# Mamba layer: the skip term as a matmul with a diagonal, row normalisation and state sum on ScalarE, another form for the low row part

## The reference, cut to what matters

```python
x = x + _L0_attn_ref(_layernorm(x), ...)
# inside: xn = (x - mu) * rsqrt(var + 1e-5) * gamma + beta; result = x + mamba_f(xn) + mamba_b(xn reversed) reversed
def _mamba(x, in_w, conv_w, conv_b, xproj_w, dt_w, dt_b, A_log, D, out_w):
    u, z = split(x @ in_w.T)
    u = silu(causal_conv4(u) + conv_b)
    x_dbl = u @ xproj_w.T                      # 8 columns dt, 16 columns B, 16 columns C
    dt = softplus(x_dbl[..., :8] @ dt_w.T + dt_b)
    A = -exp(A_log)
    h[t] = exp(dt*A) * h[t-1] + dt * B * u     # per channel and state n
    y[t] = sum_n h[t, n] * C[t, n] + u * D     # u * D is the skip term
    return (y * silu(z)) @ out_w.T
```

## Time and profile before

| | us |
|---|---|
| median of 3 runs | 2815.53 |
| lowest and highest | 2811.09, 2817.47 |
| the profiled execution, device time | 2811.5 |
| its span in the trace | 2809.7 |
| Mamba layer in it | about 24 to 1137 |

### The profile page before, as it was taken

The page is one execution under the profiler, slowest core; times in us unless marked ns, Lnnn a source line. Parts: engine busy times, 40 slices in busy tenths (PEclk is TensorE's granted clock), DMA queues, the critical chain, the costliest instruction groups (busy, mean ns, idle before and its releaser), DMA issues. The chain is left out here.

```text
span 2809.7 us, 46598 instructions
## 1 busy us (share of the span) xinstructions
PE 2401.2 (85%) x14880; PEld 1568.5 (56%) x14880; DVE 2138.4 (76%) x3085; ACT 1455.2 (52%) x2617; POOL 1191.9 (42%) x864
## 2 busy tenths in 40 slices
PE   2778878778887877799779999699999989978997
PEld 0233333333333332577578888466666767767776
DVE  3899999999999999577555555588888867764555
ACT  2666666666666774466332222466666646642010
POOL 4566667666666667333300000455555533231000
PEclk9899999999999999899789999899999999988999
DMA  2000000000000000200000000000000010000000
GB/s 84 1 0 0 1 0 1 1 1 0 0 0 0 0 1 0 63 12 12 22 1 1 1 0 0 6 0 0 0 0 0 1 48 11 11 4 1 11 7 12
DMA packets 35414, 22.17 MB, mean 8 GB/s; under 512 B 22710, under 2 KB 34017, under 8 KB 34801
## 3 DMA queue, kind: packets, MB, share of 16 engines
q1 hardware_dynamic: 35312, 20.98, 2.9%
HBM read 18.87 MB, written 2.10 MB: 7 GB/s over the span
## 5 line engine op out<-in xcount | busy, mean ns | idle before, releaser
L784 POOL TENSOR_TENSOR m_hc<-m_h,m_cs 128x1024 f32<-128x1024 f32 x256 | 603.2, 2359 | 351.9 <-DVE m_h L706 344.6
L706 DVE TENSOR_TENSOR_SCAN m_h<-m_da,m_pdb 128x1024 f32<-128x1024 f32 x256 | 585.1, 2286 | 23.5 <-DVE m_pdb L661 5.0
L456 PE MATMUL m_py<-m_hc,ident 128*128 128x512 f32 x1024 | 514.6, 627 | 4.2 <-DVE m_y L670 2.1
L579 ACT ACTIVATE m_da<-m_dt,m_aneg 128x508 f32<-128x508 f32 x512 | 337.8, 709 | 47.8 <-POOL m_dt L753 46.1
L661 DVE TENSOR_TENSOR m_pdb<-m_du,m_pdb 128x1024 f32<-128x1024 f32 x256 | 314.8, 1230 | 42.7 <-POOL m_du L760 11.4
L456 PEld LDWEIGHTS m_py<-m_hc,ident 128*128 128x128 f32 x1024 | 202.2, 200 | 213.6 <-issue 174.6
L594 ACT ACTIVATE m_cs<-m_pc 128x512 f32<-128x512 f32 x256 | 150.5, 588 | 219.7 <-PE m_pc L446 219.6
L442 PE MATMUL m_pdb<-m_bcrow,m_sel 96*128 96x512 bf16 x256 | 101.8, 397 | 171.8 <-DVE m_h L706 170.8
L1391 ACT ACTIVATE c_act_of<-c_pg 128x512 f32<-128x512 f32 x144 | 86.2, 598 | 237.3 <-PE c_pg L212 237.3
L1759 POOL TENSOR_TENSOR d_pr<-d_pr,d_rden 128x512 f32<-128x512 f32 x128 | 133.3, 1041 | 177.2 <-DVE d_rden L1690 177.2
L1037 ACT ACTIVATE x_prT<-x_pt 77x512 f32<-77x512 f32 x256 | 137.8, 587 | 130.6 <-PE x_pt L939 129.5
(11 more groups left out here) (257 smaller groups left out, 5373.7 us busy)
## 6 DMA issues: line engine op xcount, KB each, us to landing
cw_gu<-in_C_gu SPq DMA_DIRECT2D x1, 2304.0 KB
x<-in_x SPq DMA_DIRECT2D x8, 256.0 KB, 4.9
fw_w<-in_F_w SPq DMA_DIRECT2D x1, 2048.0 KB
out_x<-x SPq DMA_DIRECT2D x8, 256.0 KB, 2.3
bm_mrow<-in_B_mrow SPq DMA_DIRECT2D x1, 1232.0 KB, 6.5
x_ctxT<-in_B_ctxT SPq DMA_DIRECT2D x32, 38.5 KB, 1.8
x_mask<-in_B_mrow SPq DMA_DIRECT2D x32, 38.5 KB, 2.8
x_ctxT<-in_E_ctxT SPq DMA_DIRECT2D x32, 38.5 KB, 1.8
```

The lines of the kernel that those rows point to most:

```text
L456: ins = mm(py[:, c, :], S.ident[:, :], hc[n % BUF][:, place(n, c), :], start=n == 0, stop=n == NS - 1)
L579: A_(dst, src, ACT.Exp, scale=aneg[:, d, c, n:n + 1]).then_inc(s["da_ready"], 1)
L706: V.tensor_tensor_scan(h[n % BUF][:, way], da[n % BUF][:, d:d + CH * GT][:, way], pdb[:, b:b + 2, :].rearrange("p c t -> p (c t)")[:, way] ...
L784: P.tensor_tensor(hc[n % BUF][:, :, :], h[n % BUF][:, :].rearrange("p (c t) -> p c t", c=CH), bc(cs[n % BUF][:, :], 1, CH), ALU.mult).then ...
```

## The change

It does five things in `mamba_layer`:
1. Four tiles `skip` (128 x 128, one for each direction and half) are made once: the identity times D. `add_state` at state 0 first multiplies `us` with them into `py` (`start=True`), and the identity matmuls behind them only add. It waits for the Silus of its unit, long done.
2. `sum_up` moves from VectorE to ScalarE and becomes two plain copies from `py` to `y1`, behind the copy of C for state 3.
3. `norm` moves from VectorE to ScalarE, behind the copy of C for state 5 (and at the start of everything for group 0), as `Identity` activations with scale and bias from tiles. GpSimd makes two more small tiles for it, `nmean` and `mr12`.
4. The low row part is written by `scalar_tensor_tensor` (times 1.0, minus) where it was `tensor_tensor` (minus), with the same operands.
5. `STEPS` grows by 2 accordingly.

```diff
-    STEPS = LN_STEPS + 7
+    STEPS = LN_STEPS + 9
...
@@ TensorE
+                pe.wait_ge(s["skip_ready"], 2 * CH)
...
-                def add_state(u, n):
+                def add_state(u, n, d):
                     pe.wait_ge(s["hc_ready"], NS * u + n + 1)
                     if n == 0:
+                        pe.wait_ge(s["silu_ready"], 3 * u + CH)
                         if due(CH * u):
                             pe.wait_ge(s["y1_ready"], CH * u)
+                        for c in range(CH):
+                            mm(py[:, c, :], skip[:, d, c, :], us[d][:, c, :], start=True, stop=False)
                     for c in range(CH):
                         ins = mm(py[:, c, :], S.ident[:, :], hc[n % BUF][:, place(n, c), :],
-                                 start=n == 0, stop=n == NS - 1)
+                                 start=False, stop=n == NS - 1)
...
@@ ScalarE
+                act.wait_ge(s["rstd"], STEPS)
+                def norm(g):
+                    if isinstance(g, int) and g == 1:
+                        act.wait_ge(s["rstd"], 2 * STEPS)
+                    if due(g):
+                        act.wait_ge(s["lnT_mm"], g)
+                    for i in range(GS):
+                        b = bass.ds(g * GS + i, 1)
+                        ins = A_(xh[:, i:i + 1, :], S.x[:, b, :], ACT.Identity, bias=mr12[:, b], scale=r12[:, b])
+                    ins.then_inc(s["xh_ready"], 1)
+                    act.wait_ge(s["xh_ready"], g + 1)
+                    for i in range(GS):
+                        b = bass.ds(g * GS + i, 1)
+                        ins = A_(S.x[:, b, :], S.x[:, b, :], ACT.Identity, bias=mr1[:, b], scale=r1p[:, b])
+                    ins.then_inc(s["xres_ready"], 1)
+
+                def sum_up(u, d):
+                    act.wait_ge(s["y_mm"], NS * (u + 1))
+                    if due(u):
+                        act.wait_ge(s["ys_ready"], u)
+                    for c in range(CH):
+                        A_(y1[:, c, :], py[:, c, :], ACT.Copy).then_inc(s["y1_ready"], 1)
...
+                    if at is None:
+                        norm(g)
...
+                    if d == 1 and at == 5 and not (isinstance(g, int) and g + 1 == NG):
+                        norm(g + 1)
...
+                        if n == 3 and not (isinstance(u, int) and u == 0):
+                            sum_up(u - 1, 1 - d)
                         if nxt:
                             nxt(n)
+                    if not nxt:
+                        sum_up(u, d)
...
@@ VectorE
+                for d in range(2):
+                    for c in range(CH):
+                        V.tensor_scalar(skip[:, d, c, :], S.ident[:, :], W.dskip[:, d, c:c + 1], None, ALU.mult
+                                        ).then_inc(s["skip_ready"], 1)
...
-                def norm(g):
...
-                        V.tensor_tensor(bcrow[d][64:96, :], rest[64:96, :], bcrow[d][64:96, :],
-                                        ALU.subtract).then_inc(s["row_ready"], 1)
+                        V.scalar_tensor_tensor(bcrow[d][64:96, :], rest[64:96, :], 1.0, bcrow[d][64:96, :],
+                                               ALU.mult, ALU.subtract).then_inc(s["row_ready"], 1)
...
-                def sum_up(u, d):
-
-                    dve.wait_ge(s["y_mm"], NS * (u + 1))
-                    if due(u):
-                        dve.wait_ge(s["ys_ready"], u)
-                    for c in range(CH):
-                        V.scalar_tensor_tensor(y1[:, c, :], us[d][:, c, :], W.dskip[:, d, c:c + 1],
-                                               py[:, c, :], ALU.mult, ALU.add).then_inc(s["y1_ready"], 1)
...
@@ GpSimd, at the start
+                    P.tensor_scalar(nmean[:, cols], mean, -1.0, None, ALU.mult).then_inc(s["rstd"], 1)
...
-                    P.tensor_tensor(mr1[:, cols], mean, r1, ALU.mult).then_inc(s["rstd"], 1)
+                    P.tensor_tensor(mr1[:, cols], nmean[:, cols], r1, ALU.mult).then_inc(s["rstd"], 1)
+                    pool.wait_ge(s["rstd"], done + LN_STEPS + 6)
+                    P.tensor_tensor(mr12[:, cols], nmean[:, cols], r12[:, cols], ALU.mult).then_inc(s["rstd"], 1)
```

More of the change, by code:

```diff
@@ L305, in mamba_layer @@
         mr1 = A.sb("mr1", [128, NB])
+        nmean, mr12 = A.sb("nmean", [128, NB]), A.sb("mr12", [128, NB])
+        skip = A.sb("skip", [128, 2, CH, 128])
         xh = A.sb("xh", [128, GS, D])
@@ L335, in mamba_layer @@
             row_mm row_hi row_rest row_mid row_ready dtrow_ready dt_mm dt_abs dt_relu dt_soft dt_ready
-            du_ready b_mm c_mm c_ready da_ready db_ready h_ready hc_ready y_mm y1_ready ys_ready o_mm
+            du_ready skip_ready b_mm c_mm c_ready da_ready db_ready h_ready hc_ready y_mm y1_ready ys_ready o_mm
             x_ready seg_zero aexp_ready""".split()
@@ L489, in scan @@
                         if n >= LAG:
-                            add_state(u, n - LAG)
+                            add_state(u, n - LAG, d)
                         elif not first:
-                            add_state(u - 1, NS + n - LAG)
+                            add_state(u - 1, NS + n - LAG, 1 - d)
                         if n == 8 and not first:
@@ L496, in scan @@
                         for n in range(NS - LAG, NS):
-                            add_state(u, n)
+                            add_state(u, n, d)
                         project_out(u, d, nxt)
@@ L611, in _ @@
                 find_batches_with_keys(nc, dve, masks)
-                dve.wait_ge(s["rstd"], STEPS)
                 par = [0]
-                def norm(g):
[L617 to L622, removed]
-                        ins = V.tensor_scalar(xh[:, i:i + 1, :], S.x[:, b, :], S.mean[:, b],
-                                              r12[:, b], ALU.subtract, ALU.mult)
-                    ins.then_inc(s["xh_ready"], 1)
-                    dve.wait_ge(s["xh_ready"], g + 1)
-                    for i in range(GS):
-                        b = bass.ds(g * GS + i, 1)
-                        ins = V.tensor_scalar(S.x[:, b, :], S.x[:, b, :], r1p[:, b], mr1[:, b],
-                                              ALU.mult, ALU.subtract)
-                    ins.then_inc(s["xres_ready"], 1)
                 def front(g, d, at=None):
                     u = 2 * g + d
-                    if at is None:
-                        norm(g)
-                    if d == 1 and at == 5 and not (isinstance(g, int) and g + 1 == NG):
-                        norm(g + 1)
                     if at in (None, 9):
@@ L695, in scan @@
                         if not first:
-                            if n == 3:
-                                sum_up(u - 1, 1 - d)
                             if n == 9:
@@ L713, in scan @@
                     if not nxt:
-                        sum_up(u, d)
                         add_out(u, g, d)
@@ L730, in _ @@
                     r1, var, mean = S.rstd[:, cols], S.var[:, cols], S.mean[:, cols]
+                    P.tensor_scalar(nmean[:, cols], mean, -1.0, None, ALU.mult).then_inc(s["rstd"], 1)
                     P.tensor_tensor(r1sq[:, cols], r1, r1, ALU.mult).then_inc(s["rstd"], 1)
-                    pool.wait_ge(s["rstd"], done + LN_STEPS + 1)
+                    pool.wait_ge(s["rstd"], done + LN_STEPS + 2)
                     P.tensor_tensor(v2[:, cols], var, r1sq[:, cols], ALU.mult).then_inc(s["rstd"], 1)
-                    pool.wait_ge(s["rstd"], done + LN_STEPS + 2)
+                    pool.wait_ge(s["rstd"], done + LN_STEPS + 3)
                     P.tensor_scalar(ve[:, cols], v2[:, cols], LN_EPS, None, ALU.add).then_inc(s["rstd"], 1)
-                    pool.wait_ge(s["rstd"], done + LN_STEPS + 3)
+                    pool.wait_ge(s["rstd"], done + LN_STEPS + 4)
                     P.tensor_tensor(r2[:, cols], ve[:, cols], S.minus_half[:, cols], ALU.pow).then_inc(s["rstd"], 1)
-                    pool.wait_ge(s["rstd"], done + LN_STEPS + 4)
+                    pool.wait_ge(s["rstd"], done + LN_STEPS + 5)
                     P.tensor_tensor(r12[:, cols], r1, r2[:, cols], ALU.mult).then_inc(s["rstd"], 1)
                     P.tensor_scalar(r1p[:, cols], r1, 1.0, None, ALU.add).then_inc(s["rstd"], 1)
-                    P.tensor_tensor(mr1[:, cols], mean, r1, ALU.mult).then_inc(s["rstd"], 1)
+                    P.tensor_tensor(mr1[:, cols], nmean[:, cols], r1, ALU.mult).then_inc(s["rstd"], 1)
+                    pool.wait_ge(s["rstd"], done + LN_STEPS + 6)
+                    P.tensor_tensor(mr12[:, cols], nmean[:, cols], r12[:, cols], ALU.mult).then_inc(s["rstd"], 1)
                 par = [0]
```

## The result

| | before | after |
|---|---|---|
| median of 7 runs, us | 2815.29 | 2825.7 |
| lowest and highest | 2809.22, 2817.47 | 2822.19, 2833.25 |
| the profiled execution (span) | 2811.5 (2809.7) | 2822.2 (2820.4) |

The ratio is 1.0044 [1.0029, 1.0058]: slower by 0.44%, outside the 0.2% that can be told from no change. The forecast was 2822.5, the range 2804 to 2834.

A forecast was written before the change was run, and what follows sets the result against it. TensorE was taken as all but the bound between states 3 and 9, VectorE in the other states. Terms summed to +7.1 us, 2818.5 on the profiled execution's footing; 4.0 more for the median gave 2822.5, range 2804 to 2834.

The forecast's parts named there:

- TensorE's stretch: From state 3's spread of B to the first matmul behind the projection out: 29.52 us, lengthened by 1.72 through the skip matmuls.
- A: Units scanning backwards, scan 1 to scan 9: TensorE's 1.72 us counts in full, seven units +12.0 us.
- B: Units scanning forwards with the row normalisation, scan 1 to 9: TensorE's chain rules, six units x -1.2 = -7.2 us.
- Rival 3: ScalarE's normalisation decides, its operands addressed by registers; at 0.6 us per activation +17, 2832.5 us; chance 0.18.
- VectorE's saving is worth nothing ahead of a wait: In A, the 1.2 us saved ahead of VectorE's wait for the projection gain nothing; waits for TensorE up some 45 us.
- Rival 2: TensorE does not bind, so VectorE's saving counts: 2775 us, or 2799 if only B came free; chance 0.13 for both.
- The state sum on ScalarE costs no stall: ScalarE's two copies end near 549.6, before TensorE comes to its state additions at 551.39: no stall.
- Low row part: In states after 9, the new form keeps the same two SBUF inputs beside GpSimd: 0 us taken, at most 0.93 for each of 15.
- Rival 1: The low row part gets free of GpSimd, 14 us less in the states after 9: -7, 2808.5 us; chance 0.17.
- 15th and last unit: 15th unit, without normalisation, waits for TensorE: +1.7 us; the last has no next unit's work on TensorE: -1.2 us.
- The start: Two more small GpSimd tiles and both normalisation halves on ScalarE before the activation at 40.44: +1.4 us.
- Unit 0 and the end: Unit 0 has B's chain without the projection out and loses a normalisation: +0.4 us; the end stays as it is.

The follow-up runs named there:

- Skip_out: The changed kernel without the skip product, so the term D*u is missing from the output: 2800.53 us beside 2815.71, ratio 0.9955.
- skip_twice: The changed kernel with the skip product made twice at the same place, each with half the diagonal: 2850.97 us, ratio 1.0133.
- skip_late: The changed kernel with the skip product issued behind the addition of state 9, in state 12, instead of at state 3: 2803.58 us, ratio 0.9957.
- second profile: Profile of the changed kernel run once more with no edit; that run measured 2824.03 us beside 2814.65, ratio 1.0036.
- low_alone: The kernel before with the low row part's rest kept in PSUM, one SBUF input, one state earlier: 2803.5 us beside 2812.49, ratio 0.997.
- late_both: The changed kernel with skip product in state 14, projection out at state 12 and the addition to x at 13: 2798.86 us, ratio 0.9944.

## Why the prediction was right

Point by point, by the prediction's own steps.
- **TensorE's stretch, A.** Predicted 31.3 us and 34.4 from scan 1 to 9; 31.25 and 34.4 to 34.5. Seven units +12.21, predicted +12.0. The stand for ScalarE at the spread of C moved along and did not shrink: 1.52 before and after. Skip_out, skip_twice and skip_late show that this path is what the time hangs on.
- **B.** Predicted 35.8 us, measured 35.5 to 36.1 (one unit 37.3 in the second profile); six units -6.35 instead of -7.2. The push by the normalisation on ScalarE, predicted 0.3: TensorE's stand there is 1.79 instead of 1.52, so 0.27. The activations came 0.39 apart, 3.32 us in all, against 0.39 and 3.3 expected; each lasts 0.48 us, overlapping the next. Rival 3, operands addressed by registers taking 0.6 us, fell with that.
- **VectorE's saving is worth nothing ahead of a wait.** Predicted +45 us of waits; it was +52, with the same result. Rival 2 fell: skip_out shows that even without the product A does not get under 32.7 us, although VectorE has 1.2 us less to do.
- **The state sum on ScalarE costs no stall.** The copies stood ready in time (481.53 to 482.61 in B, TensorE's product of state 0 at 484.51). skip_out, which holds them, has A at 229.23, within 0.3 of before.
- **Low row part.** Predicted 0, and 1558 ns in the mean before and after. Rival 1 fell; low_alone shows what getting free is worth, 11.65 us in its profile and 9.0 in the medians, but by another edit.
- **15th and last unit.** +1.7 and -1.2 predicted, +1.71 and -1.14 measured.
- **The start** was oversized: scan 1 came 0.1 and 0.4 us later, not 1.4. The activation of the earlier trace rows at 40.44 did come 1.13 us later, at 41.57; the way to scan 1 gave most of it back. In the first profile TensorE reached its higher level earlier within the 16 passes of the first taps, which took 7.50 us instead of 8.11 (7.89 in the second), and before alone has a stand of 0.52 us ahead of scan 1. Neither was in the sum; the first is the clock's, what the second waited for is not shown.
- **Unit 0 and the end.** The +0.4 of unit 0 is right where the clock is alike (+0.5 and +0.6, above); the table's -2.25 sets taps of 2.75 us beside taps of 5.31. The end was put at 0 and came to +0.61 and +1.05: the last projection took 2.99 and 3.43 us instead of 2.05, at a granted clock of 0.65 and 0.53 where before had 1.00.
- **From the layer to the time.** The sum said +7.1; the medians differ by +10.4 and +9.4. The layer gave +4.8 and +9.9 in the two profiles, 7.3 in the mean. That this is so near to 7.1 is in part luck: the start came 1.0 to 1.3 us under its term, the end 0.6 to 1.0 over and B 0.9 to 2.0 over, and unit 0 went once with the clock and once against it. The rest came behind the layer, +5.3 and +4.2 against the shortest stretch that any profile shows. One profiled execution stands for the median only to some 4 us here, and the step from it to the forecast, 4.0 us added because before's median lay that far above its profile, fits: the changed kernel's lies 3.5 above.

## What to carry to other kernels

Before giving an engine more work, find its own stretch between two waits, not its busy share: TensorE idled a fifth of this loop and had nothing to spare where the two matmuls were put, so 1.72 us x 15 came out in full; nine states further on the same work was free. Ask first where the engine waits, place the work there, and give the result time to arrive: one state between projection and addition was too short at either clock level, two were enough at both. The step with two SBUF inputs beside a busy GpSimd got short by moving one input to PSUM (0.69 us), not by another ALU form (1.61).

## What the runs showed of the hardware

- ScalarE's activations of 128 columns with both scale and bias from tiles last 482 ns each and come 0.39 us apart when queued (1.64 us for four); `Identity` in place of VectorE's `tensor_scalar` needed no new table load: none stands between 488.57 and 494.20 in B, and the layer has as many as before.
- TensorE's clock differs between executions of one kernel at one place: 1.00 or 0.51 over the taps of unit 0. With it unit 0 differs by 2.8 us, a quarter of the change's effect. Over the five later layers a mean granted clock of 0.942 or 0.934 goes with 1420.8 or 1432.4 us for the same instructions.
- In late_both the state addition and the projection in state 12 met the lower level in twelve of 14 units, which the projection in state 8 did not in the change (1.95 us in each of its 15 places in the loop): in the unit shown the addition of a state took 3.07 us instead of 1.88, after 6 us (505 to 511) in which TensorE was busy for 2.79.
- VectorE's `tensor_tensor` of 32x512 takes 1.61 us with two inputs in SBUF while GpSimd multiplies, ending 0.54 us behind GpSimd's product; 0.68 with GpSimd idle; 0.69 with one input in PSUM and GpSimd busy.
